# State scan with the C row copied to SBUF by ScalarE and one of four channel blocks' C products made on GpSimd

## What is computed

```
delta = softplus(xz[:, :128] @ W_dt.T + b_dt)        # per token and channel
dA    = exp(delta[..., None] * A)                    # 16 states
Bu    = delta[..., None] * B_mat[:, :, None, :] * x[..., None]
h_t   = dA_t * h_(t-1) + Bu_t                        # the scan over the 512 tokens
y_t   = sum over the 16 states of h_t * C_t          # C_t: one number per token and state
out   = y + x * D_param
```

## Time and profile before

| | us |
|---|---|
| median of three runs (2179.08 to 2182.07) | 2179.1 |
| the profiled execution, its time | 2183.05 |
| the profiled execution, its span | 2181.3 |
| busy: TensorE matmul | 1892.6 |
| busy: VectorE | 1391.5 |
| busy: ScalarE | 981.1 |
| busy: GpSimd | 768.4 |

### The profile page before, as it was taken

The page is one execution under the profiler, slowest core; times in us unless marked ns, Lnnn a source line. Parts: engine busy times, 40 slices in busy tenths (PEclk is TensorE's granted clock), DMA queues, the critical chain, the costliest instruction groups (busy, mean ns, idle before and its releaser), DMA issues. The chain is left out here.

```text
span 2181.3 us, 27455 instructions
## 1 busy us (share of the span) xinstructions
PE 1892.6 (87%) x9210; PEld 1251.2 (57%) x9210; DVE 1391.5 (64%) x2192; ACT 981.1 (45%) x1684; POOL 768.4 (35%) x1109
## 2 busy tenths in 40 slices
PE   6978664898999898897999899799899999799795
PEld 3446443695448564595447655486446666388442
DVE  4765698464663799475654599576554499666312
ACT  1412773362322795263242598164141398255031
POOL 1146366442210265462120156382120146472201
PEclk9979655997999999998999999999799999899898
DMA  6337100000213176011023076111022257210683
GB/s 242 114 105 242 56 1 0 1 2 20 96 44 116 63 263 215 11 30 41 39 102 102 29 240 223 63 40 35 27 78 100 68 184 264 83 40 21 256 295 104
DMA packets 55024, 221.09 MB, mean 101 GB/s; under 512 B 6240, under 2 KB 6240, under 8 KB 46944
## 3 DMA queue, kind: packets, MB, share of 16 engines
q1 hardware_dynamic: 45728, 195.14, 25.8%
q0 software_dynamic: 5120, 16.78, 2.3%
q10 hardware_dynamic: 4032, 7.34, 0.9%
HBM read 179.65 MB, written 39.58 MB: 101 GB/s over the span
## 5 line engine op out<-in xcount | busy, mean ns | idle before, releaser
L1888 POOL TENSOR_TENSOR Y<-Y,HC 128x1024 f32<-128x1024 f32 x120 | 283.0, 2359 | 218.1 <-DVE HC L1315 218.1
L1304 DVE TENSOR_TENSOR_SCAN HS<-DA,ps 128x1024 f32<-128x1024 f32 x128 | 292.5, 2285 | 23.8 <-PE ps L724 13.5
L1658 ACT ACTIVATE DA<-DL,AB,AN 128x511 f32<-128x511 f32 x256 | 193.8, 807 | 14.8 <-DVE HS L1304 13.5
L932 PE MATMUL ps<-ring,XBT 128*128 128x512 f32 x384 | 189.0, 599 | 0.0
L1762 ACT ACTIVATE PD<-ps,NMX 128x128 f32<-128x128 f32 (+3 forms) x256 | 134.4, 528 | 93.9 <-DVE NMX L1451 89.5
L513 PE MATMUL ps<-ring,XNT 128*128 128x512 f32 x384 | 172.7, 608 | 2.1 <-ACT VA L1605 2.1
L1451 DVE TENSOR_REDUCE NMX<-ps 128x1 f32<-128x128 f32 (+3 forms) x256 | 124.9, 489 | 72.4 <-PE ps L785 71.7
L803 PE MATMUL ps<-V,PTD 128*128 128x33 f32 x1280 | 163.9, 261 | 0.0
L803 PEld LDWEIGHTS ps<-V,PTD 128*128 128x128 f32 x1280 | 162.5, 192 | 0.0
L632 PE MATMUL ps<-XNH,tern 128*128 128x512 f32 x352 | 140.0, 398 | 9.9 <-DVE tern L1204 5.2
L1315 DVE TENSOR_TENSOR HC<-HS,ps 128x1024 f32<-128x1024 f32 x120 | 143.2, 1196 | 0.0
(11 more groups left out here) (233 smaller groups left out, 3968.2 us busy)
## 6 DMA issues: line engine op xcount, KB each, us to landing
ring<-experts_dram SPq DMA_DIRECT2D x48, 1024.0 KB, 5.1
tern<-tern_q SPq DMA_DIRECT2D x33, 768.0 KB, 4.2
ring<-experts_dram SPq DMA_DIRECT2D x48, 512.0 KB, 5.5
RAW<-tern_dram SPq DMA_DIRECT2D x22, 768.0 KB, 5.0
ring<-wqkv_dram SPq DMA_DIRECT2D x4, 3072.0 KB, 10.2
XB<-xg SPq DMA_DIRECT2D x42, 256.0 KB, 3.6
yg<-YB SPq DMA_DIRECT2D x42, 256.0 KB, 4.9
tern_q<-tern SPq DMA_DIRECT2D x11, 768.0 KB, 7.0
```

Source lines behind the costliest of these rows:

```text
L932: last = pe.matmul(ps[:, g_bank(b)], XBT[:, b % 2, k], weights(b)[:, k * C:(k + 1) * C], start=(k == 0), stop=(k == NK - 1), skip_group_ch ...
L1304: v.tensor_tensor_scan(HS[:, q].rearrange("p j t -> p (j t)"), DA[:, q].rearrange("p j t -> p (j t)"), ps[:, 2 * q:2 * q + 2].rearrange("p ...
L1658: s.activation(DA[:, u % 2, jj, 1:T], DL[:, j, 1:T], ACT.Exp, scale=AN[:, j * NS + n:j * NS + n + 1], bias=AB[:, j * NS + n:j * NS + n + 1 ...
L1888: p.tensor_tensor(y, y, HC[:, q], ALU.add).then_inc(c_y, 1)
```

## The change

ScalarE copies the C row of each state from PSUM to SBUF, into one of two buffers CR. TensorE may make the next row as soon as the copy is done. VectorE reads the copy in place of PSUM: still 128x1024 for the even unit, but only block 2 (128x512) for the odd one. GpSimd makes the product of block 3 (128x512) itself, ahead of its sum of the odd unit. VectorE's scan of the next odd unit then waits for GpSimd's product too.

```diff
+    CR = (at("CR0", [P, T], F32, "tern", 16 * KB), at("CR1", [P, T], F32, "arena", 48 * KB))
...
         def pe_C_row(pe, n):
...
             else:
-                pe.wait_ge(c_hc, 2 * n)
+                pe.wait_ge(c_crow, n)
...
         def pe_scan(pe, experts):
...
                 if n + 1 < NS:
                     pe_C_b(pe, 2 * n + 2)
-                if n:
-                    pe_C_row(pe, n)
+                    pe_C_row(pe, n + 1)
...
         def v_C_scan(v, u):
-            q = u % 2
+            n, q = divmod(u, 2)
...
             if u >= 2:
                 v.wait_ge(c_hc, u - 1)
+                if q:
+                    v.wait_ge(c_hp, n)
...
         def v_C_out(v, u):
             n, q = divmod(u, 2)
-            v.wait_ge(c_rowC, n + 1)
+            v.wait_ge(c_crow, n + 1)
...
-            dst = Y[:, 2 * q:2 * q + 2] if n == 0 else HC[:, q]
-            v.tensor_tensor(dst, HS[:, q], ps[:, 4:5, :].to_broadcast([P, 2, T]), ALU.mult).then_inc(c_hc, 1)
+            if q:
+
+                dst = Y[:, 2] if n == 0 else HC[:, 1, 0]
+                v.tensor_tensor(dst, HS[:, 1, 0], CR[n % 2][:], ALU.mult).then_inc(c_hc, 1)
+            else:
+                dst = Y[:, 0:2] if n == 0 else HC[:, 0]
+                v.tensor_tensor(dst, HS[:, 0], CR[n % 2][:].rearrange("p (o t) -> p o t", o=1).to_broadcast([P, 2, T]),
+                                ALU.mult).then_inc(c_hc, 1)
...
+        def s_C_crow(s, n):
+            s.wait_ge(c_rowC, n + 1)
+            if n == 0:
+                s.wait_ge(c_bt, 1)
+            if n >= 2:
+                s.wait_ge(c_hp, n - 1)
+                s.wait_ge(c_hc, 2 * n - 2)
+            s.copy(CR[n % 2][:], ps[:, 4]).then_inc(c_crow, 1)
...
         def s_scan(s, experts):
...
             for i in range(NT):
                 s_C_ub(s, 1, i)
+            s_C_crow(s, 0)
             for m in range(1, NS):
...
                 s_C_decay(s, 2 * m)
+                s_C_crow(s, m)
                 if done:
                     block_ht(s, s.copy, n - 2)
...
         def p_C(p, experts):
             p_split(p, experts)
+            def product(n):
+                p.wait_ge(c_scan, 2 * n + 2)
+                p.wait_ge(c_crow, n + 1)
+                if n >= 2:
+                    p.wait_ge(c_y, 2 * n - 2)
+                dst = Y[:, 3] if n == 0 else HC[:, 1, 1]
+                p.tensor_tensor(dst, HS[:, 1, 1], CR[n % 2][:], ALU.mult).then_inc(c_hp, 1)
+
+            product(0)
             for u in range(2, 2 * NS):
-                q = u % 2
+                n, q = divmod(u, 2)
+                if q:
+                    product(n)
                 p.wait_ge(c_hc, u + 1)
+                if q:
+                    p.wait_ge(c_hp, n + 1)
```

More of the change, by code:

```diff
@@ L404, in build @@
         c_hc = sem("c_hc")
+        c_crow = sem("c_crow")
+        c_hp = sem("c_hp")
         c_y = sem("c_y")
```

## The result

The changed kernel takes 2208.2 us (median of 4 runs, 2201.38 to 2210.17) beside 2180.6 for the kernel before: a ratio of 1.0118, 95% interval 1.0092 to 1.0145, so 1.2% or some 26 us slower (the two medians lie 27.6 apart). The profiled execution took 2210.17 us, its span is 2208.4.

What follows compares the result with a forecast made beforehand. VectorE was taken to pace the first scan, with TensorE and ScalarE close behind in the other three. First scan 7.7 plus 13.8 for the others made 21.5 us on 2179.1, stated as 2200.5; range 2187 to 2217.

Steps and rivals of the forecast that it cites:

- The new wait and the port, first scan: First scan: odd scan waits for GpSimd's product, itself held at the VectorE-GpSimd port; 7.55 us a state against 7.064, +6.8.
- Before the first T: First scan, before the first counted odd unit's scan start (T): no sum yet, so the cheaper product gains 0.5 us.
- The tail: From the last odd scan's start to the end of the four L1402: 12.1 us against 10.64, +1.4 in each scan.
- The copy on ScalarE: With experts, the copy ahead of HBT delays it 0.19 us a round, after a 2.1 us late start: +3.2 a batch.
- GpSimd keeps its turn: Rival, chance 0.2: at the port GpSimd's product goes before VectorE's half product; 7.67 us a state, 8.2 with experts; 2215.
- The full product from SBUF: VectorE's even-unit product from the SBUF copy was taken to cost the same as from PSUM, 1.20 us.
- The row's earlier issue: On TensorE, making the C row earlier removes a wait for VectorE; it costs nothing and gives nothing.

Runs made afterwards that it cites:

- the row-from-PSUM kernel: Changed kernel with VectorE reading the C row from PSUM again, ScalarE copying row m-1 in round m behind the decays; 2201.3 us, ratio 1.0088.
- the copy alone behind the decays: Kernel before plus ScalarE's sixteen copies per scan, which nothing reads though VectorE's products wait for them; 2199.8 us, ratio 1.0076.
- the kernel with the row made earlier: Changed kernel, row from PSUM, product ahead of even sum, copy ahead of XBT, TensorE's row between the expert block's first two products; 2177.6 us, ratio 0.998.

## Why the prediction was right, and where it was off

The direction, and both mechanisms, were right: 21.5 us was forecast, 26 measured (the ratio's interval is 20 to 32 us), 26.5 by scans in the profiles: 10.0 for 7.7 in the first scan, 16.5 for 13.8 in the others. That the second pair lies so close is partly luck, as shown under the copy.

*The new wait and the port, first scan.* The chain was named as it runs. Its size was off: 7.55 us a state forecast, 7.694 measured. The term that failed is GpSimd's product: 1.15, or 1.0 after a wait. Its free duration in this place is 1.27 (the row-from-PSUM kernel), and with the half product's hold it is 1.75 from its start, so that it ends 1.13 us after the half product, where I had 1.0. The half product itself did not wait at all. It asks at 280.30, and sum 2n, which ends at 280.39, lets it in without delay: 0.67 us, as long as alone. So the port cost is GpSimd's, 0.48 us a state, and the rest of the loss is the chain: 7.187 without the port, where I had 7.03, against 7.064 before. The sharing alone, without the port conflict, would have gained nothing, as forecast. From first to last T it is +8.8 for +6.8.

*Before the first T.* In the first scan -0.2 for -0.5: the scans of units 2 and 3 waited 0.34 and 0.24 us for their decays, behind the copy.

*The tail.* 12.06 us for 12.1, four times. Here the port sum was exact. The sums and the last product, after; the first sum waits at first for the half product, which began 0.16 us before it:

```profile
370.37 2.72 POOL L1922 TENSOR_TENSOR Y<-Y,HC 128x1024 f32<-128x1024 f32 x1 [1.16 <-DVE HC L1324]
373.05 1.26 POOL L1909 TENSOR_TENSOR HC<-HS,CR 128x512 f32<-128x512 f32 x1
374.44 2.61 POOL L1922 TENSOR_TENSOR Y<-Y,HC 128x1024 f32<-128x1024 f32 x1
```

*The copy on ScalarE.* Forecast +3.2 a scan with experts from first to last scan; measured 4.8, 2.9 and 4.5 (table, first two columns). The start of the term was exact: the first HBT comes 2.1 us later in its scan than before (21.4 us after the first scan's start for 19.3). The step that failed is the delay of 0.19 us a round. TensorE's rounds are 7.85, not 7.94, beside 7.78 before; HBT's copy started 0.66 us ahead of its matmul before and 0.46 after, so it had some 0.2 us in hand, not 0.05. The last transposes of the third batch end 2.9 us later in the scan than before, not 4.4, and no late scan waits for them. What holds the scans up there is the chain and the port: most odd scans wait 0.48 us for GpSimd's product, 7.72 us a state in place of 7.634, 1.2 us in 14 states. TensorE's slower rounds come in through ScalarE's decays, for which even scans wait some 0.25 us, until VectorE is late enough for the next paragraph's case; in the third batch two states pay some 0.6 us each for that. These two make up most of its 2.7 us. The second and the fourth batch pay 1.8 and 1.5 us more, by a fall of the clock that the prediction does not have; without these 3.4 us the three scans would have lost 13 us, near the 13.8 forecast, but by other terms. Of the copy's price, moving it off HBT's path gave back 1.5 us where the clock held in both kernels (the third batch, 109.54 to 108.0) and 1.3 to 1.7 where it fell in both.

*GpSimd keeps its turn.* This rival, with a chance of 0.2, came true in 4, 2 and 4 of the 14 states of the three scans with experts, and in none of the first scan. In these VectorE asked late, because its even scan had been held up by its decays. VectorE, then GpSimd, with experts:

```profile
789.39 2.29 DVE L1308 TENSOR_TENSOR_SCAN HS<-DA,ps 128x1024 f32<-128x1024 f32 x1 [0.36 <-ACT DA L1668]
791.59 1.66 DVE L1321 TENSOR_TENSOR HC<-HS,CR 128x512 f32<-128x512 f32 x1
...
799.68 0.67 DVE L1321 TENSOR_TENSOR HC<-HS,CR 128x512 f32<-128x512 f32 x1
```

```profile
791.42 1.28 POOL L1909 TENSOR_TENSOR HC<-HS,CR 128x512 f32<-128x512 f32 x1
...
799.74 1.74 POOL L1909 TENSOR_TENSOR HC<-HS,CR 128x512 f32<-128x512 f32 x1
```

At 791.42 GpSimd starts first: 1.28 and 1.66. At 799.68 VectorE does, by 0.06 us: 0.67 and 1.74. Who starts first decides, which is what the Trainium skill says ("SBUF — State Buffer", the section on who interferes with whom); the rows agree. From T to T a state of the first kind takes 8.3 to 8.4 us, one of the second 7.7.

*The full product from SBUF.* 1.20 us (1.23 where it meets the end of a sum), as assumed. The 0.065 us that the table of the Trainium skill cited in the prediction ("VectorE: DVE Perf Modes", the section on the TRN2 errata) would take off did not show: the product from PSUM took 1.19 to 1.20.

*The row's earlier issue.* Taken as nothing. No experiment changed it alone; the wait that it brings (0.99 to 1.0 us of ScalarE for the row, in the first scan) delayed no scan that I can see.

## What to carry to other kernels

Before work is moved off the busiest engine, follow one period of the loop through the waits that the move adds: here the freed 0.53 us was wholly taken by a chain through the helper, and two-input SBUF instructions on both engines cost 0.5 more. Moved work pays when the new chain is cut, the shared port is kept free (here by reading one input from PSUM) and an instruction added to a third engine (here the copy) stands in a gap, with its input ready before the gap opens. Where the engines behind the busiest one are full too, as with experts here, leave the stage alone and change only the stage that has room.

## What the runs showed that I had not expected

The second and fourth batches lost 1.8 and 1.5 us more than the third. TensorE's wait for the first HBT is equally long in all three, 2.01 us; in the second and the fourth the granted clock then fell to 0.50, which is 1.2 GHz, and the down products took 3.48 and 2.60 us in place of 1.98. TensorE in the second and the third batch, then the granted clock of three stretches of the second (column before the last two) and of one in the third:

```profile
772.71 3.48 PE L959 MATMUL ps<-ring,HBT 128*128 128x512 f32 x4 [2.01 <-ACT HBT L1379]
...
1283.51 1.98 PE L959 MATMUL ps<-ring,HBT 128*128 128x512 f32 x4 [2.01 <-ACT HBT L1379]
```

```profile
772.00:775.00 3.00, 2.29 (x3) 0.68 0.74 300
774.00:775.00 1.00, 1.00 (x2) 0.50 0.76 320
775.00:778.00 3.00, 3.00 (x13) 0.76 0.31 34
...
1282.70:1285.70 3.00, 2.19 (x8) 1.00 0.80 314
```

The stretches at 0.68 and 0.76 lie partly at 1.2 and partly at 2.4 GHz. In the kernel before, the trace has 0.57 us of waiting there in each of the three batches, and the clock holds.

The other runs bear on it, though none was made for it. The wait of 2.0 us for HBT stands in all nine scans with experts of the changed kernel, of the one with the product ahead of the sum and of the one without GpSimd's product, and the clock fell behind it in eight of them. With the copy in the gap, TensorE's row waits for the copy instead: 1.91 us in the changed kernel, with a fall in two scans of three, and 1.65 us without GpSimd's product, with a fall in one. In the kernels with the row from PSUM and with the copy alone behind the decays, TensorE waits 2.0 to 3.0 us for VectorE's first products, and the clock fell in three scans of six. In the kernel with the row made earlier it waits 2.1 to 2.6 us there, and the clock held in all three. So a copy that makes one instruction late can cost its own delay and then a second time as slower matmuls, 0.9 to 1.8 us a scan between fall and no fall of one kernel. Which waits are followed by a fall is not shown: the same length has both outcomes.

The time outside the scans differs by up to 10 us between profiled executions (1672.7 to 1682.6 us over these kernels, the same code), more than several effects here. The comparison scan by scan, which repeats to 0.1 us where the clock does the same, is what tells them apart.
